# Cell passes of a four-layer graph network: visits past a group's second, one at a time with one-hots 128 wide

## The chip, the cores and the metric

The kernel runs on one core of a Trainium2 chip. The metric is the device time of one execution in microseconds (us).

## The reference

Four graph layers follow each other on 12,500 nodes with 64 features and 200,000 edges sorted by destination; each adds its result to `x`. Every layer gathers the rows of the edges' sources and sums them by destination. Layer 2 (GraphSAGE) does it twice, layer 3 (GCN) once, and these three sums are the subject here:

```python
dst = jnp.minimum((12500 * jax.random.uniform(..., (200000,)) ** 2.0).astype(jnp.int32), 99999)
# sorted; src goes along
...
def _sage_layer(h, src, dst, W_self, W_neigh, b, n_nodes):
    msg = h[src]
    agg = jax.ops.segment_sum(msg, dst, num_segments=n_nodes)
    deg = jax.ops.segment_sum(jnp.ones((src.shape[0], 1), h.dtype), dst, num_segments=n_nodes)
    h_neigh = agg / jnp.maximum(deg, 1.0)
    return h @ W_self + h_neigh @ W_neigh + b
...
msg = norm[:, None] * h[row]                             # layer 3
agg = jax.ops.segment_sum(msg, col, num_segments=N)
```

Since the destinations follow a square law, low nodes have many edges each and high nodes few.

## The kernel before

Layers 0 and 1 are worked by two edge passes, then `cells_setup` sorts the edges of each group by source page, and three **cell passes** (`cell_pass`) do the sums of layers 2 and 3. A cell pass goes over 75 groups (`CELLS`) of 2,688 edges. The nodes are cut into 98 windows of 128. A group has 26 tiles of 128 edge slots: 25 filled by a gather with one-hot matrices from `split` in SBUF, and one (`spill`) fetched by GpSimd's indirect DMA.

For each window that a group's destinations touch there is one **visit**: TensorE (PE) multiplies 26 one-hot tiles (slot by node of the window) with the 26 tiles of gathered rows (192 columns, a value split in three bf16 parts) into one PSUM bank (`segment`, line 1216), and VectorE (DVE) reduces the three parts (`reduce_visit`, line 1223) and adds them to the window of `agg` (`add_visit`, line 1228). Cutting the sorted destinations of the reference into groups of 2,688 gives in each pass 15 groups with one visit, 28 with two, 27 with three and 5 with four: 172 visits. The groups with three or four stand in the later part of the pass: counted from 0, groups 51 to 73 all have at least three. The five with four are groups 62, 66, 69, 71 and 73.

The one-hots are made on DVE by `build`: one small instruction for the places (line 1308), then 25 (`SLOT_TILES`) comparisons with fp8 output (line 1312) and one with bf16 output for the spill tile (line 1314). `lanes` counts from 0 to 255, so one build is 256 wide and serves two neighbouring windows, `half` 0 and 1. Buffers 0 and 1 hold the one-hots for a group's first and second visit, in turn by group; buffer 2 those for its third and fourth. In the first cell pass (`make`) DVE builds buffers 0 and 1 and SyncE (SP) stores them to HBM (`pairs_d`); the other two passes load them from there. Buffer 2 is always built anew.

Each engine has its own loop over the groups, two groups to an iteration (`over_rounds`), with the group's words in registers: `low` and `end` (the windows), `more` (the extra visits of all groups before) and `pairs`, from the table `sched`. The order on DVE for group g is: buffer 2 for g if `low + 2 < end`; in the first pass, the one-hots of group g+1; then the first visit's reduce and add, the second's under `If(low + 1 < end)`, and a `Fori` over the others in steps of two. PE works through the gather of group g+1 and the first visit of group g tile by tile in turn (line 1370 and line 1216), then the second visit, then its own `Fori`. The visits write PSUM banks in this way: the first `ps_first[k]`, the second and the fourth `ps_extra[0]`, the third `ps_extra[1]`. ScalarE (ACT) moves gathered rows from PSUM to SBUF (line 1286).

PE's third visit waits for `s_hot_more` (buffer 2 is built) and `s_add_more` (the bank is reduced); its fourth waits for `s_add_more` alone, since its one-hots lie in the other half of buffer 2.

Of the kernel before, what the change touches and what calls it, by code (L numbers as in the profile page):

```python
# [23 lines left out]
ALU = mybir.AluOpType  # L24
# [3 lines left out]
P = 128  # L28
NODES, EDGES, D = 12500, 200000, 64
WINDOWS = -(-NODES // P)  # L30
# [47 lines left out]
def build(nc, a):  # L78

    ctx = ExitStack()  # L80
    with ctx:
# [96 lines left out]
        def reach(eng, s, value):  # L178

            hold(eng, s, value & COUNTS)  # L180
# [580 lines left out]
        def cells_setup():  # L761
# [62 lines left out]
            with nc.Block() as block:  # L824
# [18 lines left out]
                def _(dve):  # L843
# [24 lines left out]
                    link(nc.vector.tensor_copy(extra[:, 0:1], high))  # L868
                    link(nc.vector.tensor_scalar(high, high, 1, 1, ALU.logical_shift_right, ALU.logical_shift_left))
                    link(nc.vector.tensor_copy(extra[:, 1:2], high))  # L870

# [259 lines left out]
        def cell_pass(start=None, bring=False, make=True):  # L1131
# [40 lines left out]
            def ranged(eng, regs, donate=True):  # L1172

                most = CELLS * (WINDOWS + 1)
                return (eng.snap(regs[0], donate=donate, min_val=0, max_val=WINDOWS - 1),
                        eng.snap(regs[1], donate=donate, min_val=1, max_val=WINDOWS),
                        eng.snap(regs[2], donate=donate, min_val=1 - WINDOWS, max_val=most),
                        eng.snap(regs[3], donate=donate, min_val=1 - WINDOWS, max_val=most))

            def over_rounds(eng, body):  # L1180
# [4 lines left out]
                def words():  # L1185

                    low, end, more, pairs = ranged(eng, regs[0:SCHED], False)
                    return low, end, more, pairs, eng.snap(regs[SCHED], min_val=0, max_val=WINDOWS - 1)

# [40 lines left out]
            with nc.Block() as block:  # L1230
# [62 lines left out]
                def _(dve):  # L1293
# [11 lines left out]

                    def build(k, g, w, placed, n_placed, signal):

                        nc.vector.tensor_scalar(place[k], slot_dst[:, bass.ds(g * SLOTS_OF, SLOTS_OF)], first[:, bass.ds(w, 1)],  # L1308
                                                1.0, ALU.subtract, ALU.subtract).then_inc(placed, 2)
                        reach(dve, placed, n_placed)  # L1310
                        for q in range(SLOT_TILES):
                            nc.vector.tensor_scalar(slots_hot[k][:, q, :], lanes[:, :], place[k][:, q:q + 1], None,  # L1312
                                                    ALU.is_equal, saturate=False)
                        last = nc.vector.tensor_scalar(spill_hot[k], lanes[:, :], place[k][:, SLOT_TILES:SLOTS_OF], None,
                                                       ALU.is_equal)
                        last.then_inc(signal, 2)

                    def add_up(of, w, k, added, signal, count):

                        reach(dve, s_add, added)  # L1320
                        reduce_visit(of, k).then_inc(signal, 1)
                        reach(dve, signal, count)
                        add_visit(w, k).then_inc(s_add, 1)

                    def body(it, r, words, following):
                        g0 = it * CELL_STEP
                        g = g0 + r
                        low, end, more, pairs, low1 = words
                        if there(it, r, 0):
                            with dve.If(low + 2 < end):  # L1330
                                build(2, g, low + 2, s_place_more, pairs + (low + 2), s_hot_more)
                        if there(it, r, 1):
# [13 lines left out]
                        with dve.If(low + 2 < end):  # L1346
                            with dve.Fori(low + 2, end, 2) as w:
                                reach(dve, s_sum_more, more + w)
                                add_up(ps_extra[1], w, 0, (more + w) + g, s_add_more, more + (w + 2))
                                with dve.If(w + 1 < end):  # L1350
                                    reach(dve, s_sum_more, more + (w + 1))
                                    add_up(ps_extra[0], w + 1, 1, (more + w) + (g0 + (r + 1)), s_add_more, more + (w + 3))
                                with dve.If(w + 2 < end):
                                    build(2, g, w + 2, s_place_more, pairs + (w + 2), s_hot_more)
                    over_rounds(dve, body)

                @block.tensor
                def _(pe):
# [17 lines left out]
                    def body(it, r, words, following):  # L1376
                        g0 = it * CELL_STEP
                        k = r % 2
                        low, end, more, pairs, _ = words
                        for c in range(n_pick):  # L1380
# [24 lines left out]
                        with pe.If(low + 2 < end):  # L1405
                            with pe.Fori(low + 2, end, 2) as w:
                                reach(pe, s_hot_more, pairs + w)
                                reach(pe, s_add_more, more + w)
                                segment(ps_extra[1], 2, 0, picked[k], rows_of, every).then_inc(s_sum_more, 1)
                                with pe.If(w + 1 < end):  # L1410
                                    reach(pe, s_add_more, more + (w + 1))
                                    segment(ps_extra[0], 2, 1, picked[k], rows_of, every).then_inc(s_sum_more, 1)

# [598 lines left out]
```

## Time and profile before

| | us |
|---|---|
| median of 3 runs | 10334.19 |
| lowest, highest | 10326.15, 10350.14 |
| the profiled execution | 10342.89 |
| its span | 10341.2 |
| DVE busy | 4747.4 |
| PE busy | 5394.1 |
| granted TensorE clock, mean | 0.681 |

The span runs from the first instruction of the program to the last. The three cell passes are roughly the stretches 7304 to 8395, 8495 to 9320 and 9475 to 10305 us of it. A busy share is a mean over stages with different limits, so what one stage is bound by is read from that stage's own rows.

### The profile page before, as it was taken

How to read it: one execution, taken by the hardware profiler on the slowest of the kernel's cores; microseconds unless marked ns; L12 is line 12 of the kernel's file. 1: busy time of each engine (PE TensorE's matmuls, PEld its weight loads, DVE VectorE, ACT ScalarE, POOL GpSimd, SP SyncE). 2: the span in 40 equal slices, each digit the busy share in tenths (PEclk: the TensorE clock that was granted, in tenths of full speed). 3: DMA queues.
4: the chain of work that ended last, by engine and by line, in shares of the span. 5: the costliest groups of instructions: out<-in, count | busy, mean ns of one | idle time of the engine just before them, and what ended most of it. 6: DMA issues, size and time to landing. Idle time of an engine off the chain costs nothing. (4 is left out here: it accounts for less than half of the span.)

```text
span 10341.2 us, 263147 instructions
## 1 busy us (share of the span) xinstructions
PE 5394.1 (52%) x94327; PEld 4139.3 (40%) x94328; DVE 4747.4 (46%) x12946; ACT 1982.3 (19%) x3084; POOL 3376.8 (33%) x3400
## 2 busy tenths in 40 slices
PE   1333233333344444444444456666776668885886
PEld 1222222222233333333333355555454455664565
DVE  3333333333533333333333377777778751463156
ACT  1111111111211111111111100000443225433542
POOL 4666666665144444444444400000111100000000
PEclk7555555555655555555555567777798879996999
DMA  2221122211122222222222112223332124322432
GB/s 74 48 47 48 47 48 49 47 47 41 35 57 59 59 59 59 59 59 60 60 59 59 49 51 81 83 82 97 117 117 79 67 76 140 122 95 104 137 116 100
DMA packets 310309, 747.47 MB, mean 72 GB/s; under 512 B 85284, under 2 KB 110500, under 8 KB 307225
## 3 DMA queue, kind: packets, MB, share of 16 engines
q1 hardware_dynamic: 175524, 610.42, 18.1%
q0 software_dynamic: 107552, 114.03, 5.5%
q10 hardware_dynamic: 26656, 16.06, 0.5%
q8 instruction: 272, 4.46, 0.2%
q14 instruction: 305, 2.50, 0.1%
HBM read 601.52 MB, written 138.69 MB: 72 GB/s over the span
## 5 line engine op out<-in xcount | busy, mean ns | idle before, releaser
L556 POOL DMA_INDIRECT store<-table,store x3136 | 3071.9, 980 | 2623.4 <-DVE store L689 1660.9
L709 PE MATMUL ps_all<-store 128*128 128x65 bf16 (+1 forms) x18816 | 1493.5, 232 | 3027.6 <-issue 2705.8
L709 PEld LDWEIGHTS ps_all<-store 128*128 128x128 bf16 x18816 | 1094.1, 122 | 3386.0 <-issue 3382.8
L1216 PE MATMUL ps_all<-store 128*128 128x192 bf16 x13416 | 1505.6, 254 | 382.3 <-DVE turned L1223 175.5
L637 DVE TENSOR_TENSOR agg<-ps_all,agg 128x130 f32 (+1 forms) x392 | 113.7, 290 | 3128.2 <-PE ps_all L709 2361.0
L1286 ACT CAST store<-ps_all 128x768 bf16<-128x768 f32 x1350 | 1063.8, 799 | 1575.6 <-PE ps_all L1370 1526.3
L1216 PEld LDWEIGHTS ps_all<-store 128*128 128x128 fp8e4 x13416 | 1074.9, 100 | 722.1 <-issue 698.7
L1312 DVE TENSOR_SCALAR store<-lanes,turned 128x256 fp8e4<-128x256 bf16 x4275 | 1138.2, 347 | 26.9 <-DVE turned L1308 21.8
L1244 POOL DMA_INDIRECT store<-table_b,spill_row x225 | 297.1, 1320 | 2277.8 <-PE ps_all L1370 2119.7
L731 PE MATMUL ps_all<-wide,store 128*128 x9408 | 538.1, 241 | 458.1 <-DVE store L644 413.3
L731 PEld LDWEIGHTS ps_all<-wide,store 128*128 128x128 bf16 x9408 | 505.4, 131 | 490.0 <-issue 489.8
L628 DVE TENSOR_SCALAR store<-lanes,place_of 128x256 bf16<-128x256 bf16 x3136 | 665.6, 297 | 62.9 <-DVE place_of L624 51.0
L1223 DVE TENSOR_REDUCE turned<-ps_all 128x64 f32<-128x192 f32 x516 | 183.1, 355 | 913.4 <-PE ps_all L1216 846.9
L600 ACT ACTIVATE store<-store 128x512 bf16<-128x512 f32 x196 | 125.2, 639 | 2163.3 <-DVE store L681 2162.0
L422 POOL MEMSET wide<- 128x384 bf16 x4 | 1.7, 418 | 1573.5 <-POOLq L1088 1216.7
L1370 PE MATMUL ps_all<-wide,store 128*32 128x192 bf16 x11172 | 413.8, 265 | 154.6 <-issue 72.9
L594 ACT CAST store<-store 128x512 bf16<-128x512 f32 x392 | 244.3, 623 | 1121.6 <-issue 686.4
L1370 PE MATMUL ps_all<-wide,turned 128*32 128x192 bf16 x10878 | 405.7, 266 | 99.1 <-issue 77.8
L644 DVE TENSOR_SCALAR store<-store,node_id 128x1024 bf16<-128x1024 int32 x392 | 277.3, 749 | 171.8 <-issue 133.3
L1370 PEld LDWEIGHTS ps_all<-wide,store 128*32 128x32 fp8e4 x11172 | 230.7, 100 | 302.3 <-issue 301.4
L1370 PEld LDWEIGHTS ps_all<-wide,turned 128*32 128x32 fp8e4 x10878 | 227.2, 101 | 246.1 <-issue 245.6
L603 ACT CAST store<-store 128x512 bf16<-128x512 f32 x196 | 122.6, 625 | 967.6 <-DVE store L684 797.7
(229 smaller groups left out, 5405.6 us busy)
## 6 DMA issues: line engine op xcount, KB each, us to landing
store<-pairs_d SPq DMA_DIRECT2D x150, 864.0 KB, 4.5
store<-in_dst_rows SPq DMA_DIRECT2D x196, 512.0 KB
pairs_d<-store SPq DMA_DIRECT2D x75, 864.0 KB, 4.0
store<-lows_d SPq DMA_DIRECT2D x75, 784.0 KB, 5.2
store<-in_edge_attr SPq DMA_DIRECT2D x196, 256.0 KB
store<-table,store POOLq DMA_INDIRECT x3136
store<-cells_d SPq DMA_DIRECT2D x114, 392.0 KB
turned<-cells_d SPq DMA_DIRECT2D x111, 392.0 KB
```

What stands on the lines that cost most here:

```text
L556: nc.gpsimd.indirect_dma_start(rows_f[:, g % SLOTS, j, :], None, table, bass.IndirectOffsetOnAxis(ap=src[:, g * TILES + j:g * TILES + j + ...
L594: nc.scalar.copy(value[slot][:, :, 1, 0:D], rows_f[:, slot, :, :]).then_inc(s_mid, 1)
L628: last = nc.vector.tensor_scalar(onehots[:, k, j, :], lanes[:, :], place[:, j:j + 1], None, ALU.is_equal)
L644: nc.vector.tensor_scalar(onehot_t[b][:, :, :].rearrange("p j e -> p (j e)"), side_i[:, slot, :], node_id[:, bass.ds(w + b, 1)], None, ALU ...
L709: last = nc.tensor.matmul(ps_pair[r % 2][:, b * width:(b + 1) * width], onehot[r % 2][b][:, j, :], value[r][:, j, i, 0:width], start=(b == ...
L731: last = nc.tensor.matmul(ps_hid[:, r % 2, j * D:(j + 1) * D], onehot_t[b][:, j, :], split[:, bass.ds(w + b, 1), i, :].rearrange("p o d -> ...
L1216: last = nc.tensor.matmul(to, hot[:, half * P:(half + 1) * P], rows[:, q, :] if q < SLOT_TILES else spill, start=(q == 0), stop=True, skip ...
L1223: return nc.vector.tensor_reduce(sums[k], of.rearrange("p (i d) -> p d i", i=PARTS), AX.X, ALU.add)
L1244: nc.gpsimd.indirect_dma_start(spill[:, g, :], None, table_b, bass.IndirectOffsetOnAxis(ap=spill_row[:, g:g + 1], axis=0)).then_inc(s_fetc ...
L1286: nc.scalar.copy(picked[r % 2][:, c * PICK:(c + 1) * PICK, :], of).then_inc(s_evicted, 1)
L1312: nc.vector.tensor_scalar(slots_hot[k][:, q, :], lanes[:, :], place[k][:, q:q + 1], None, ALU.is_equal, saturate=False)
L1370: last = nc.tensor.matmul(ps_pick[(r + 1 + c) % 2][j * CAP:(j + 1) * CAP, q, 0:PARTS * D], gather_hot[k][:, w * CAP:(w + 1) * CAP], split[ ...
```

## The change

Visits past the second are worked one by one. `build` takes a width: with `n=1` each of its 26 comparisons makes 128 columns in place of 256, for one window. On DVE, buffer 2 is built so for the third visit, and after the add of visit `w` it is built again for `w + 1` if there is one. All visits past the second use the bank `ps_extra[1]` and `half` 0. The `Fori` of both engines goes in steps of one, PE's loop has no `If` inside, and DVE's has one in place of two. The word `pairs` becomes `lone`, a count of such visits, and `cells_setup` works it out in one instruction fewer.

```diff
--- before.py
+++ after.py
@@ -866,8 +866,7 @@
                     link(nc.vector.tensor_scalar(columns[:, 1:2], high, 1.0, None, ALU.add))
                     link(nc.vector.tensor_tensor(high, high, low, ALU.subtract))
                     link(nc.vector.tensor_copy(extra[:, 0:1], high))
-                    link(nc.vector.tensor_scalar(high, high, 1, 1, ALU.logical_shift_right, ALU.logical_shift_left))
-                    link(nc.vector.tensor_copy(extra[:, 1:2], high))
+                    link(nc.vector.tensor_scalar(extra[:, 1:2], extra[:, 0:1], 1.0, 0.0, ALU.subtract, ALU.max))
 
             s_target = sem("s_c_target")
             s_cell, s_sums, s_summed, s_prefix, s_top, s_over, s_rank, s_rank_hot, s_slots = (sem(f"s_c_{n}") for n in (
@@ -1184,8 +1183,8 @@
 
                 def words():
 
-                    low, end, more, pairs = ranged(eng, regs[0:SCHED], False)
-                    return low, end, more, pairs, eng.snap(regs[SCHED], min_val=0, max_val=WINDOWS - 1)
+                    low, end, more, lone = ranged(eng, regs[0:SCHED], False)
+                    return low, end, more, lone, eng.snap(regs[SCHED], min_val=0, max_val=WINDOWS - 1)
 
                 def following(it, r):
                     def load():
@@ -1303,17 +1302,17 @@
                         nc.vector.memset(agg[:, WINDOWS:PAIR_END, :], 0.0)
                         nc.vector.tensor_copy(agg[:, 0:WINDOWS, 0:D], start[:, :, :]).then_inc(s_add, 1)
 
-                    def build(k, g, w, placed, n_placed, signal):
+                    def build(k, g, w, placed, n_placed, signal, n=2):
 
                         nc.vector.tensor_scalar(place[k], slot_dst[:, bass.ds(g * SLOTS_OF, SLOTS_OF)], first[:, bass.ds(w, 1)],
-                                                1.0, ALU.subtract, ALU.subtract).then_inc(placed, 2)
+                                                1.0, ALU.subtract, ALU.subtract).then_inc(placed, n)
                         reach(dve, placed, n_placed)
                         for q in range(SLOT_TILES):
-                            nc.vector.tensor_scalar(slots_hot[k][:, q, :], lanes[:, :], place[k][:, q:q + 1], None,
+                            nc.vector.tensor_scalar(slots_hot[k][:, q, 0:n * P], lanes[:, 0:n * P], place[k][:, q:q + 1], None,
                                                     ALU.is_equal, saturate=False)
-                        last = nc.vector.tensor_scalar(spill_hot[k], lanes[:, :], place[k][:, SLOT_TILES:SLOTS_OF], None,
-                                                       ALU.is_equal)
-                        last.then_inc(signal, 2)
+                        last = nc.vector.tensor_scalar(spill_hot[k][:, 0:n * P], lanes[:, 0:n * P],
+                                                       place[k][:, SLOT_TILES:SLOTS_OF], None, ALU.is_equal)
+                        last.then_inc(signal, n)
 
                     def add_up(of, w, k, added, signal, count):
 
@@ -1325,10 +1324,10 @@
                     def body(it, r, words, following):
                         g0 = it * CELL_STEP
                         g = g0 + r
-                        low, end, more, pairs, low1 = words
+                        low, end, more, lone, low1 = words
                         if there(it, r, 0):
                             with dve.If(low + 2 < end):
-                                build(2, g, low + 2, s_place_more, pairs + (low + 2), s_hot_more)
+                                build(2, g, low + 2, s_place_more, lone + (low + 1), s_hot_more, 1)
                         if there(it, r, 1):
                             if make:
                                 k = (r + 1) % 2
@@ -1344,14 +1343,11 @@
                             reach(dve, s_sum_more, more + (low + 1))
                             add_up(ps_extra[0], low + 1, 1, (more + low) + (g0 + (r + 1)), s_add_more, more + (low + 3))
                         with dve.If(low + 2 < end):
-                            with dve.Fori(low + 2, end, 2) as w:
+                            with dve.Fori(low + 2, end) as w:
                                 reach(dve, s_sum_more, more + w)
-                                add_up(ps_extra[1], w, 0, (more + w) + g, s_add_more, more + (w + 2))
+                                add_up(ps_extra[1], w, 0, (more + w) + (g0 + (r + 1)), s_add_more, more + (w + 2))
                                 with dve.If(w + 1 < end):
-                                    reach(dve, s_sum_more, more + (w + 1))
-                                    add_up(ps_extra[0], w + 1, 1, (more + w) + (g0 + (r + 1)), s_add_more, more + (w + 3))
-                                with dve.If(w + 2 < end):
-                                    build(2, g, w + 2, s_place_more, pairs + (w + 2), s_hot_more)
+                                    build(2, g, w + 1, s_place_more, lone + w, s_hot_more, 1)
                     over_rounds(dve, body)
 
                 @block.tensor
@@ -1376,7 +1372,7 @@
                     def body(it, r, words, following):
                         g0 = it * CELL_STEP
                         k = r % 2
-                        low, end, more, pairs, _ = words
+                        low, end, more, lone, _ = words
                         for c in range(n_pick):
                             if there(it, r, 1):
                                 gather(it, r, c)
@@ -1403,13 +1399,10 @@
                             reach(pe, s_add_more, more + (low + 2))
                             segment(ps_extra[0], k, 1, picked[k], rows_of, every).then_inc(s_sum_more, 1)
                         with pe.If(low + 2 < end):
-                            with pe.Fori(low + 2, end, 2) as w:
-                                reach(pe, s_hot_more, pairs + w)
-                                reach(pe, s_add_more, more + w)
+                            with pe.Fori(low + 2, end) as w:
+                                reach(pe, s_hot_more, lone + (w - 1))
+                                reach(pe, s_add_more, more + (w + 1))
                                 segment(ps_extra[1], 2, 0, picked[k], rows_of, every).then_inc(s_sum_more, 1)
-                                with pe.If(w + 1 < end):
-                                    reach(pe, s_add_more, more + (w + 1))
-                                    segment(ps_extra[0], 2, 1, picked[k], rows_of, every).then_inc(s_sum_more, 1)
 
                     over_rounds(pe, body)
```

The rows below are instructions in the order of the program on one engine. Line numbers are each kernel's own: 1308, 1312 and 1314 of before (places, fp8 and bf16 comparisons) are 1307, 1311 and 1313 of the change, 1216 is 1215, and 1223 and 1228 are 1222 and 1227. The first two pieces are DVE's loop over the visits past the second, from the last add in it to the loop's end. Before:

```order
L1228 TENSOR_TENSOR agg<-turned,agg 128x64
L1350 UNCONDITIONAL_BRANCH
L1353 COMPARE_AND_BRANCH
L1308 ISA
L1308 TENSOR_SCALAR turned<-wide,first 128x26
L175 REGISTER_ALU x2
L1312 TENSOR_SCALAR store<-lanes,turned 128x256 x25
L1314 TENSOR_SCALAR store<-lanes,turned 128x256
L1353 UNCONDITIONAL_BRANCH
L1347 REGISTER_ALU
L1347 COMPARE_AND_BRANCH
```

And of the change, from the only add in the loop:

```order
L1227 TENSOR_TENSOR agg<-turned,agg 128x64
L1349 REGISTER_ALU
L1349 COMPARE_AND_BRANCH
L1307 ISA
L1307 TENSOR_SCALAR turned<-wide,first 128x26
L175 REGISTER_ALU x2
L1311 TENSOR_SCALAR store<-lanes,turned 128x128 x25
L1313 TENSOR_SCALAR store<-lanes,turned 128x128
L1349 UNCONDITIONAL_BRANCH
L1346 REGISTER_ALU
L1346 COMPARE_AND_BRANCH
```

Two branches, each with a jump of its own, stood behind the third visit's add (L1350 ahead of the fourth visit, L1353 ahead of a build for a fifth and sixth); one is left (L1349), and the build behind it is 128 wide and is now reached for a fourth visit.

The same loop on PE, before (L1370 is the next group's gather, L1410 the inner condition):

```order
L1405 COMPARE_AND_BRANCH
L1406 UNCONDITIONAL_BRANCH
L1406 ISA
L175 REGISTER_ALU x3
L1216 MATMUL ps_all<-store 128x192 x26
L1410 REGISTER_ALU
L1410 COMPARE_AND_BRANCH
L175 REGISTER_ALU x2
L1216 MATMUL ps_all<-store 128x192 x26
L1410 UNCONDITIONAL_BRANCH
L1406 REGISTER_ALU
L1406 COMPARE_AND_BRANCH
```

And of the change:

```order
L1401 COMPARE_AND_BRANCH
L1402 UNCONDITIONAL_BRANCH
L1402 ISA
L175 REGISTER_ALU
L175 ISA
L175 REGISTER_ALU
L1215 MATMUL ps_all<-store 128x192 x26
L1402 REGISTER_ALU
L1402 COMPARE_AND_BRANCH
```

One block of 26 matmuls is left, with the loop's branch right behind it; a fourth visit goes round the loop and waits for both semaphores again.

## Rows read from the trace of the kernel before

**Rows 1.** The page's head: the span.

```profile
span 10341.2 us, 263147 instructions
```

**Rows 2.** Busy us (x instructions) of PE, PEld, DVE, ACT, POOL; clock; DMA; GB/s.

```profile
7304.00:8395.00 1091.00, 769.61 (x11778) 536.39 (x11774) 851.51 (x3234) 379.54 (x524) 151.56 (x72) 0.87 0.27 91
8495.00:9320.00 825.00, 686.77 (x11632) 490.41 (x11628) 324.25 (x1208) 368.42 (x515) 63.36 (x68) 0.97 0.36 117
9475.00:10305.00 830.00, 688.76 (x11668) 491.88 (x11665) 324.27 (x1208) 370.29 (x516) 63.37 (x68) 0.97 0.36 117
```

**Rows 3.** Timeline, first cell pass, three-visit groups: start, us, engine, line [idle before].

```profile
8094.30 0.35 DVE L1223 TENSOR_REDUCE turned<-ps_all 128x64 f32<-128x192 f32 x1
...
8099.59 0.24 DVE L1308 TENSOR_SCALAR turned<-wide,first 128x26 f32 x1 [1.87 <-issue]
...
8106.75 0.23 DVE L1308 TENSOR_SCALAR turned<-wide,first 128x26 f32 x1
...
8113.90 0.34 DVE L1223 TENSOR_REDUCE turned<-ps_all 128x64 f32<-128x192 f32 x1
```

**Rows 4.** Timeline, second cell pass, three-visit groups, DVE and PE.

```profile
9091.50 2.31 PE L1216 MATMUL ps_all<-store 128*128 128x192 bf16 x26 [0.81 <-DVE store L1314]
...
9093.99 0.51 PE L1370 MATMUL ps_all<-wide,turned 128*32 128x192 bf16 x16 [0.18 <-issue]
...
9094.94 0.23 DVE L1228 TENSOR_TENSOR agg<-turned,agg 128x64 f32 x1 [0.24 <-DVE turned L1223]
...
9097.12 0.24 DVE L1308 TENSOR_SCALAR turned<-wide,first 128x26 f32 x1 [1.95 <-issue]
...
9104.09 0.28 DVE L1314 TENSOR_SCALAR store<-lanes,turned 128x256 bf16<-128x256 bf16 x1
...
9104.88 2.31 PE L1216 MATMUL ps_all<-store 128*128 128x192 bf16 x26 [1.17 <-DVE store L1314]
```

**Rows 5.** Waits of PE for the builds, second pass, then third: us, times, longest.

```profile
PE ps_all L1216 <- DVE store L1314: 24.3, 22, 1.5
...
PE ps_all L1216 <- DVE store L1314: 22.2, 22, 1.4
```

**Rows 6.** Timeline, second cell pass, a group with four visits.

```profile
9157.07 4.45 PE L1216 MATMUL ps_all<-store 128*128 128x192 bf16 x52 [1.17 <-DVE store L1314]
...
9160.40 0.23 DVE L1228 TENSOR_TENSOR agg<-turned,agg 128x64 f32 x1 [0.24 <-DVE turned L1223]
...
9161.45 0.51 PE L1370 MATMUL ps_all<-wide,store 128*32 128x192 bf16 x16
```

**Rows 7.** Timeline, first cell pass, a group with four visits.

```profile
8154.30 4.32 PE L1216 MATMUL ps_all<-store 128*128 128x192 bf16 x26 [5.96 <-DVE turned L1223]
...
8155.79 0.23 DVE L1228 TENSOR_TENSOR agg<-turned,agg 128x64 f32 x1 [0.24 <-DVE turned L1223]
...
8159.63 0.23 DVE L1228 TENSOR_TENSOR agg<-turned,agg 128x64 f32 x1 [0.24 <-DVE turned L1223]
```

**Rows 8.** Busy and clock while that group's fourth visit runs.

```profile
8154.20:8158.60 4.40, 4.30 (x30) 3.72 (x34) 0.81 (x3) 0.00 (x0) 0.00 (x0) 0.50 0.69 242
```

**Rows 9.** Durations by line (ns min/median/max), whole run; L959 is of the setup.

```profile
L1312 DVE TENSOR_SCALAR store<-lanes,turned x4275: 334/347/492, 7305.8 to 10287.3; 128x256 fp8e4<-128x256 bf16 x195
...
L1314 DVE TENSOR_SCALAR store<-lanes,turned x171: 270/279/327, 7312.5 to 10287.6; 128x256 bf16<-128x256 bf16 x171
...
L959 DVE TENSOR_SCALAR store<-store,next_id x75: 1845/1853/1855, 6088.8 to 7217.2; 128x3136 fp8e4<-128x3136 bf16 x75
```

**Rows 10.** Branches: DVE's at one group's end in the second pass; PE's, whole run.

```profile
L1353 DVEq COMPARE_BRANCH  x1: 123/123/123, 9095.4 to 9095.4; - x1
...
L1347 DVEq ALU_OP  x1: 45/45/45, 9095.8 to 9095.8; - x1
...
L1330 DVEq ALU_OP  x1: 40/40/40, 9096.7 to 9096.7; - x1
...
L1405 PEldq COMPARE_BRANCH  x225: 71/216/1780, 7322.3 to 10297.6; - x113
```

## The prediction

> **What bounds the kernel now.** The page's head gives the span, 10341.2 us [rows 1]; the profiled execution took 10342.89, the median of the three runs is 10334.19. The change touches the three cell passes alone, so I first read the busy times of those three stretches [rows 2]: 1091, 825 and 830 us long. In the first DVE is busy for 852 us, in the other two PE for 687 and 689 and DVE for only 324. So the same edit has two different backgrounds.
>
> In the first pass the timeline of DVE [rows 3] shows two builds end to end (8099.59 to 8106.75 and on to 8113.9) and a period of 8113.90 - 8094.30 = 19.60 us in three-visit groups. The one large gap, 1.87, is "issue": branches and register work, no wait for PE. DVE sets this pass, and a us off its builds is a us off the pass.
>
> In the other two passes a period is 9104.88 - 9091.50 = 13.38 us [rows 4]. Here the chain goes through both engines: PE's third visit starts when the build has ended (9104.09 + 0.28 = 9104.37, PE at 9104.88: 0.51 later), DVE adds it at 9094.94, reaches its next build 2.18 us later at 9097.12, and builds for 7.25 us. But PE idles only 0.81 and 1.17 us for it. What a faster build can give here is bounded by that idle time, not by the build. The waits of PE for L1314 are 24.3 us in 22 times in the second pass and 22.2 in 22 in the third [rows 5].
>
> **The narrower build.** A comparison with fp8 output takes 347 ns for 256 columns; the same kind of instruction over 3,136 columns takes 1853 [rows 9]. That is 1506/2880 = 0.523 ns a column, so most of the 347 is not columns: 128 fewer take off 67 ns, not half. The bf16 one takes 279, which is 68 less for the same 256 columns, so its columns cost half as much: 33 ns off. One build: 25 x 67 + 33 = 1.71 us less, 7.25 becomes 5.54. No row has an fp8 comparison 128 wide. The bounds are no saving at all, and half of the distance between starts (7.16 us for the 27 instructions of a build in rows 3 is 0.265 each), 3.4 us a build. I take 1.71, because two independent row pairs give the same slope. The Trainium skill ("VectorE: DVE Perf Modes", section on the TRN2 errata) speaks against cutting builds up: a fixed cost is paid per instruction whatever its size. The trace agrees as to the kind (0.523 ns a column under a 347 ns instruction of 256). The page's formula, 58 cycles + columns over the mode's factor, would make 128 fp8 columns 127 ns; that is an estimate from the page, and by it the whole sum would be some 26 us lower, since each fourth build would be 1.7 us shorter. The rows' fixed part is larger than that, and the rows decide.
>
> There are 32 such builds a pass. **First pass:** 32 x 1.71 = 54.7 us off. The second branch behind the add goes too: L1353 starts at 9095.4, the next record at 9095.8 [rows 10], I take 0.35: 32 x 0.35 = 11.2 off. PE does not become the bound there: it idles for DVE by several us a group.
>
> **Second and third pass:** PE's idle time before third visits vanishes. Each listed wait is under the 1.71 (longest 1.5), so all of 46.5 us in 44 waits goes, and a little more: 52 matmuls of two visits with no wait between take 4.45 us [rows 6], 26 take 2.31, so an unhindered visit starts 0.17 before the modelled end of the one ahead: 44 x 0.17 = 7.5. The other 20 waits are too short to be listed; I estimate 0.3 each, 6. Together 60 off. PE's inner condition costs something only in every second group: the next gather starts 0.18 after the third visit's end [rows 4], against 0.07 before the end where no jump is taken (9161.45 against 9157.07 + 4.45) [rows 6]: 27 x 0.25 = 7 off. Then PE alone is the bound.
>
> **The fourth visit.** Five groups a pass lose what the wide build gave them: one-hots ready for the fourth visit. Now the chain is: third add, a build, PE, the add, with nothing beside it, and PE's queue holds the whole next group behind its wait.
>
> *First pass.* Before, the third add starts at 8155.79 and the fourth at 8159.63: 3.84 [rows 7]. After: from the add to the build 0.48 (register work begins with the add, and L1330's, at 9096.7, leads to L1308 at 9097.12 [rows 4, 10]), the build 5.54, hand-over to PE 0.51, the visit 4.32, to the add 1.01 (8154.30 + 4.32 to 8159.63 [rows 7]): 11.86. That is 8.0 more, 5 x 8.0 = 40. PE's lateness hides behind the two builds that follow. First pass in all: -54.7 - 11.2 + 40 = -25.9.
>
> *Second and third.* Before, with the third visit at S = 9157.07, the next gather starts at S + 4.38 and the third add at S + 3.33 [rows 6]. After: fourth visit on PE at S + 3.33 + 0.48 + 5.54 + 0.51 = S + 9.86. By then PE has idled 7.5 us. In the first pass an idle time of 5.96 us was followed by a visit of 4.32 us [rows 7] at a granted clock of 0.50 [rows 8], that is at 1.2 GHz, where one at 2.4 GHz takes 2.31. So I take the low level here too, though these passes now hold 0.97 in the mean [rows 2]: 4.32 - 0.16 of overlap, and 0.25 for the gather's first tiles. The next gather starts at S + 14.3, 9.9 late; PE is the bound, so nothing hides it: 10 x 9.9 = 99.
>
> **The sum.** -25.9 - 60 - 7 + 99 = +6 us against the profiled 10342.89, and as much against the median: 10334 + 6 = 10340. The rest (one setup instruction less, fewer words of program) is nothing. Three numbers of opposite signs nearly cancel, so the forecast is no change that can be measured.
>
> **Rivals.**
> *PE gets back less than its idle time (slower).* A gather starts 0.18 us after a third visit with nothing but branches ahead of it [rows 4]. If a third visit kept that gap behind the second in place of 0.17 of overlap, 64 x 0.35 = 22 of the 60 stay lost: +28, 10362. Against it: with only the bank to wait for, two visits ran with no gap [rows 6]. Chance 0.14. It decides once more than 0.23 a visit stays lost.
> *The loop's back edge stalls (slower).* The loop now goes round, 15 times on each engine. A branch of PE took up to 1780 ns [rows 10]. At that price on the chain: 15 x 1.7 = 25, 10365. Against it: the median branch is 216 ns, and PE's sequencer meets the back edge while it must wait for the build anyway. The Trainium skill ("Runtime: NRT & Kernel Launch", section on instruction fetch) says that a taken branch to a page outside the fetched window stalls for a fetch; no row here tells where pages lie. Chance 0.09.
> *The narrow comparison is not shorter in spacing (slower).* Then 54.7 + 60 are not gained and 15 builds cost 1.7 more: 6 + 115 + 25 = +146, 10480. Two row pairs speak against it. Chance 0.04.
> *The fourth visit is cheaper (faster).* If PE stays at 2.4 GHz in its fourth visits, 15 x 2.2 = 33 fall away: -27, 10307. If the spacing halves, 47 builds are 1.7 shorter where it counts: -78, 10260. The clock rows speak against the first, the slope against the second. Chance 0.14.
>
> **How the numbers follow.** The sum as worked out has a chance of 0.59, and by its own terms lies within 25 us of 10340. A change of 0.2% (21 us) is about what this measurement can tell from none. Of the 0.59, 0.46 lies within that, 0.10 above, 0.03 below. With the rivals: faster 0.03 + 0.12 = 0.15; slower 0.10 + 0.12 + 0.07 + 0.04 = 0.33; same 0.52. The range reaches down to the clock rival and up past the two small slow ones, with the runs' own scatter (10326 to 10350): 10305 to 10385; beyond lie the two builds' extremes.
>
> **What the next profile should show.** L1311 at 280 ns and L1313 near 246, 200 ns apart; the first pass 26 us shorter, the second and third 14 and 18 longer, between them three-visit periods of some 12 us with PE never idle for a build, and in the 10 four-visit groups a hole of 7.5 us on PE with 0.50 behind it. Wrong would be: PE still idle before third visits, no hole or a longer one, or a first pass as long as before.

## The result

| | us |
|---|---|
| median of the changed kernel, 4 runs | 10512.73 |
| lowest, highest | 10505.1, 10526.6 |
| median of the kernel before beside it, 4 runs | 10342.17 |
| ratio, 95% interval | 1.0168, 1.0149 to 1.0186 |
| span of the profiled execution | 10503.4 (before 10341.2) |

The change makes the kernel slower by 1.7%, some 170 us, where no change was forecast. These are the three cell passes of the changed kernel, with the busy us of each engine as in [rows 2]:

```profile
7300.00:8480.00 1180.00, 770.63 (x11782) 553.53 (x11774) 824.42 (x3369) 377.19 (x524) 75.29 (x72) 0.84 0.25 84
8580.00:9450.00 870.00, 695.94 (x11649) 497.59 (x11638) 299.50 (x1345) 368.82 (x515) 63.45 (x68) 0.95 0.35 113
9603.00:10468.00 865.00, 688.54 (x11647) 493.64 (x11644) 297.21 (x1343) 369.58 (x515) 63.45 (x68) 0.96 0.34 112
```

DVE is busy for less in each pass (824 against 852, 300 against 324, 297 against 324), and yet each is longer. I measure a pass from its first add of a visit to its last. These are the adds of before, first pass, and of the changed kernel's three passes (count, ns, first and last start in us):

```profile
L1228 DVE TENSOR_TENSOR agg<-turned,agg x172: 224/226/295, 7323.1 to 8389.3; 128x64 f32 x172
```

```profile
L1227 DVE TENSOR_TENSOR agg<-turned,agg x172: 224/226/293, 7319.4 to 8474.6; 128x64 f32 x172
...
L1227 DVE TENSOR_TENSOR agg<-turned,agg x172: 224/226/291, 8583.9 to 9443.4; 128x64 f32 x172
...
L1227 DVE TENSOR_TENSOR agg<-turned,agg x172: 224/226/230, 9607.4 to 10462.2; 128x64 f32 x172
```

So the passes take 1155.2, 859.5 and 854.8 us, against 1066.2, 817.7 and 819.2 before: +89, +42 and +36, 166 together, where the spans differ by 162. Forecast were -26, +14 and +18.

The timeline of the first pass shows where the time goes. Here is a group with three visits, DVE and PE (beside [rows 3]):

```profile
8064.73 0.24 DVE L1313 TENSOR_SCALAR store<-lanes,turned 128x128 bf16<-128x128 bf16 x1
8064.90 0.23 DVE L1307 TENSOR_SCALAR turned<-wide,first 128x26 f32 x1
...
8073.27 0.36 DVE L1222 TENSOR_REDUCE turned<-ps_all 128x64 f32<-128x192 f32 x1 [0.42 <-DVE agg L1227]
...
8073.78 3.80 PE L1215 MATMUL ps_all<-store 128*128 128x192 bf16 x26 [6.92 <-DVE turned L1222]
...
8078.00 0.36 DVE L1222 TENSOR_REDUCE turned<-ps_all 128x64 f32<-128x192 f32 x1 [3.89 <-PE ps_all L1215]
```

The narrow one-hots are ready at 8064.97, and PE's third visit starts at 8073.78. What releases it is DVE's second reduce at 8073.27, which stands behind the build of the next group's one-hots. By then PE has idled 6.92 us, the third visit takes 3.80 us in place of 2.31, and DVE waits 3.89 for it, in a pass in which DVE is the bound. All 32 third visits of this pass look like that: PE idles 6.6 to 8.3 us ahead of each and takes 3.6 to 4.3 for it. The second pass has the same wait in small, beside [rows 4]:

```profile
9160.03 2.31 PE L1215 MATMUL ps_all<-store 128*128 128x192 bf16 x26 [0.39 <-issue]
9160.74 0.25 DVE L1313 TENSOR_SCALAR store<-lanes,turned 128x128 bf16<-128x128 bf16 x1
...
9162.60 0.36 DVE L1222 TENSOR_REDUCE turned<-ps_all 128x64 f32<-128x192 f32 x1 [0.87 <-PE ps_all L1215]
9163.10 1.07 PE L1215 MATMUL ps_all<-store 128*128 128x192 bf16 x11 [0.76 <-DVE turned L1222]
```

The build is over at 9160.99, before PE is done with the second visit at 9162.34, as forecast; but PE idles 0.76 us all the same, again until a second reduce. These are PE's waits of the second pass, as in [rows 5]:

```profile
PE ps_all L1215 <- DVE store L1313: 37.4, 5, 7.5
PE ps_all L1366 <- ACT store L1285: 24.7, 57, 0.6
PE ps_all L1215 <- DVE turned L1222: 24.4, 32, 0.8
```

The 22 waits for a build are gone; 5 are left, those of the fourth visits, 7.5 us each. In their place stand 32 waits for L1222, one for each third visit, 24.4 us, as much as before.

The reason is in the diff, and the prediction went past it. `s_add_more` begins at 2 and counts the reduces of all extra visits (those past a group's first), and `more + low` is the number of those of earlier groups. PE's third visit, w = low + 2, waited for `more + w`, which needs nothing of its own group. In the change it waits for `more + (w + 1)`: one reduce of its own group, the second visit's. The one bank does not ask for that, since the second visit has another. (A second count in the diff moves by one as well: DVE's third reduce now waits for the second visit's add, where `(more + w) + g` was the first visit's. That one costs nothing: from the second add to the third reduce it is 8039.24 - 8038.45 = 0.79 us before and 8164.03 - 8163.24 = 0.79 in e1 below, which has the new count.)

### The profile page after: what moved, and what is told of

It is laid out like the page before. It is cut to its first block and busy times, and to the rows that moved or that the text cites. A ratio compares the mean times of both kernels' runs of the same rounds, so it can differ in the third digit from the quotient of the medians.

```text
span 10503.4 us, 263458 instructions
## 1 busy us (share of the span) xinstructions
PE 5394.3 (51%) x94327; PEld 4158.3 (40%) x94328; DVE 4665.0 (44%) x13350; ACT 1980.2 (19%) x3084; POOL 3287.3 (31%) x3400
## 5 line engine op out<-in xcount | busy, mean ns | idle before, releaser
L1215 PE MATMUL ps_all<-store 128*128 128x192 bf16 x13416 | 1546.6, 259 | 534.7 <-DVE turned L1222 309.1
L1215 PEld LDWEIGHTS ps_all<-store 128*128 128x128 fp8e4 x13416 | 1117.1, 102 | 873.4 <-issue 841.7
L1311 DVE TENSOR_SCALAR store<-lanes,turned 128x128 fp8e4<-128x128 bf16 (+1 forms) x4650 | 1053.0, 306 | 29.0 <-DVE turned L1307 23.6
L1243 POOL DMA_INDIRECT store<-table_b,spill_row x225 | 220.8, 981 | 2431.6 <-PE ps_all L1366 2273.3
L1222 DVE TENSOR_REDUCE turned<-ps_all 128x64 f32<-128x192 f32 x516 | 183.2, 355 | 1182.8 <-PE ps_all L1215 1155.0
```

The lines of the kernel that those rows point to most:

```text
L1215: last = nc.tensor.matmul(to, hot[:, half * P:(half + 1) * P], rows[:, q, :] if q < SLOT_TILES else spill, start=(q == 0), stop=True, skip ...
L1222: return nc.vector.tensor_reduce(sums[k], of.rearrange("p (i d) -> p d i", i=PARTS), AX.X, ALU.add)
L1243: nc.gpsimd.indirect_dma_start(spill[:, g, :], None, table_b, bass.IndirectOffsetOnAxis(ap=spill_row[:, g:g + 1], axis=0)).then_inc(s_fetc ...
L1311: nc.vector.tensor_scalar(slots_hot[k][:, q, 0:n * P], lanes[:, 0:n * P], place[k][:, q:q + 1], None, ALU.is_equal, saturate=False)
```

## The experiments

Ratios are to runs of the kernel before beside each experiment: median 10385.4 us for e1, e2, e3 and e6, and 10333.0 for e4, e5 and e7. The two sets differ outside the cell passes: there (the span less the three passes) the profiled executions of before, the changed kernel, e4, e5 and e7 spend 7633 to 7638 us, those of the other four 7678 to 7694. So the passes are compared, measured as above.

| kernel | ratio to before | 95% interval | passes, us |
|---|---|---|---|
| before | | | 1066.2, 817.7, 819.2 |
| the changed kernel | 1.0168 | 1.0149 to 1.0186 | 1155.2, 859.5, 854.8 |
| e1_loose_wait | 0.9988 | 0.9978 to 0.9999 | 1040.0, 835.0, 829.0 |
| e2_tight_wait | 1.0186 | 1.0169 to 1.0202 | 1179.1, 859.7, 860.2 |
| e3_narrow_by_need | 0.9932 | 0.9918 to 0.9947 | 1042.9, 798.0, 798.3 |
| e4_busy_before_fourth | 0.9986 | 0.9977 to 0.9995 | 1036.7, 826.9, 823.8 |
| e5_busy_before_third | 1.0120 | 1.0104 to 1.0136 | 1102.9, 861.8, 861.6 |
| e6_no_fifth | 0.9961 | 0.9946 to 0.9975 | 1060.9, 807.0, 809.5 |
| e7_narrow_two_branches_less | 0.9929 | 0.9915 to 0.9943 | 1033.8, 792.3, 796.5 |

A pass differs by 2 to 7 us even where a run changes nothing in it (e5's second and third against the changed kernel's). The period of a group is steadier: from the start of the last add of one group to that of the next, worked out from the 172 adds of each pass, mean of groups 51 to 73 (18 with three visits, 5 with four), in us for the first, second and third pass:

| kernel | three visits | four visits |
|---|---|---|
| before | 19.18, 12.91, 12.80 | 23.00, 15.07, 15.04 |
| the changed kernel | 20.70, 12.67, 12.68 | 32.33, 23.85, 23.90 |
| e1_loose_wait | 17.23, 11.80, 11.78 | 28.81, 23.20, 23.26 |
| e2_tight_wait | 22.90, 14.36, 14.40 | 25.44, 16.56, 16.50 |
| e3_narrow_by_need | 18.16, 11.95, 11.93 | 23.10, 15.25, 15.22 |
| e4_busy_before_fourth | 17.23, 11.76, 11.72 | 27.20, 21.24, 21.31 |
| e5_busy_before_third | 19.07, 12.67, 12.69 | 30.88, 23.95, 24.06 |
| e6_no_fifth | 18.85, 12.49, 12.45 | 22.72, 14.64, 14.66 |
| e7_narrow_two_branches_less | 17.85, 11.81, 11.84 | 23.00, 14.87, 14.86 |

### The wait alone taken back: e1_loose_wait

Against the changed kernel:

```diff
                                 reach(pe, s_hot_more, lone + (w - 1))
-                                reach(pe, s_add_more, more + (w + 1))
+                                reach(pe, s_add_more, more + w)
```

> The changed kernel with one edit: in TensorE's loop over the visits past the second, the wait on s_add_more is for more + w instead of more + (w + 1), so a third visit no longer waits until the group's second visit has been reduced (a fourth is still held back until the third is reduced, by the wait for its one-hots). Theory (the extra wait is what the prediction missed): all other terms of the prediction then hold, +6 us on the kernel before, ratio 1.000 within 0.003; first pass about 26 us shorter than before's 1066, second and third 14 and 18 longer than 818 and 819, and no idle time of TensorE before third visits in those two. Rival (the extra fourth builds and the low clock behind them are the loss): the time stays within 30 us of the changed kernel, ratio at 1.013 or more.

Measured: 0.9988. The first pass is 26.2 us shorter than before (forecast 25.9), the second and third are 17.3 and 9.8 longer (forecast 14 and 18). On the timeline, a third visit of the second pass:

```profile
9109.70 0.24 DVE L1307 TENSOR_SCALAR turned<-wide,first 128x26 f32 x1 [1.51 <-issue]
9110.09 4.99 DVE L1311 TENSOR_SCALAR store<-lanes,turned 128x128 fp8e4<-128x128 bf16 x25 [0.16 <-DVE turned L1307]
...
9114.33 4.45 PE L1215 MATMUL ps_all<-store 128*128 128x192 bf16 x52 [0.34 <-issue]
9115.00 0.24 DVE L1313 TENSOR_SCALAR store<-lanes,turned 128x128 bf16<-128x128 bf16 x1
```

Second and third visit run as one block of 52 matmuls. The theory stands and its rival falls: a count that is off by one is the whole loss. Pass by pass the changed kernel is 115, 25 and 26 us over e1, together 166.

### The wait alone put in: e2_tight_wait

Against the kernel before:

```diff
                                 reach(pe, s_hot_more, pairs + w)
-                                reach(pe, s_add_more, more + w)
+                                reach(pe, s_add_more, more + (w + 1))
```

> The kernel before with only the opposite edit: its third visit waits for more + (w + 1), that is for the reduce of the second visit. One-hots, banks and loops stay as before. Theory of the extra wait: in the first pass VectorE then waits some 3.6 us in each of 32 groups for a third visit that starts only after its second reduce, +115 us; in the others TensorE's third visit starts 1.5 us later on the chain, 32 x 1.5 = +48 each; together +210, ratio 1.020. Rival: ratio within 0.003 of 1.

Measured: 1.0186. The passes are 113, 42 and 41 us longer, 196 together (forecast 115, 48 and 48); a three-visit group of the second pass takes 1.45 us more (forecast 1.5). In the first pass, with wide one-hots and two banks:

```profile
8073.35 0.36 DVE L1223 TENSOR_REDUCE turned<-ps_all 128x64 f32<-128x192 f32 x1 [0.42 <-DVE agg L1228]
8073.86 4.32 PE L1216 MATMUL ps_all<-store 128*128 128x192 bf16 x26 [9.24 <-DVE turned L1223]
8073.96 0.23 DVE L1228 TENSOR_TENSOR agg<-turned,agg 128x64 f32 x1 [0.25 <-DVE turned L1223]
8078.60 0.36 DVE L1223 TENSOR_REDUCE turned<-ps_all 128x64 f32<-128x192 f32 x1 [4.41 <-PE ps_all L1216]
```

It is the same picture as in the changed kernel: the loss needs neither the narrow build nor the single bank nor the new loop.

### The narrow build where there is no fourth visit: e3_narrow_by_need

Against the kernel before (`build` takes the width `n` as in the change):

```diff
                             with dve.If(low + 2 < end):
-                                build(2, g, low + 2, s_place_more, pairs + (low + 2), s_hot_more)
+                                with dve.If(low + 3 < end):
+                                    build(2, g, low + 2, s_place_more, pairs + (low + 2), s_hot_more)
+                                with dve.If(end < low + 4):
+                                    build(2, g, low + 2, s_place_more, pairs + (low + 2), s_hot_more, 1)
```

> The kernel before, where buffer 2 is built 128 wide if the group has three visits and 256 wide, as before, if it has four. The banks, waits and the fourth visit are those of before. It has what the narrow build gives without the second build: first pass 27 x 1.71 = 46 us off, less some 0.4 us of branches in each of 32 groups, other passes 27/32 of 60 = 50 off: -83, ratio 0.992. If the narrow build is worth nothing on the chain: 1.001.

Measured: 0.9932. Each pass is shorter, by 23, 20 and 21 us: 64, where 83 were forecast (33 in the first, 50 in the others). On the first pass's timeline, first e3, then the kernel before:

```profile
8055.97 0.24 DVE L1308 TENSOR_SCALAR turned<-wide,first 128x26 f32 x1 [2.53 <-issue]
...
8071.82 0.23 DVE L1228 TENSOR_TENSOR agg<-turned,agg 128x64 f32 x1 [0.24 <-DVE turned L1223]
8074.02 0.24 DVE L1308 TENSOR_SCALAR turned<-wide,first 128x26 f32 x1 [1.97 <-issue]
8074.41 4.99 DVE L1312 TENSOR_SCALAR store<-lanes,turned 128x128 fp8e4<-128x128 bf16 x25
...
8079.48 0.23 DVE L1308 TENSOR_SCALAR turned<-wide,first 128x26 f32 x1
```

```profile
8041.34 0.24 DVE L1308 TENSOR_SCALAR turned<-wide,first 128x26 f32 x1 [1.27 <-issue]
```

The build takes 8079.48 - 8074.02 = 5.46 us to the next, as it should. What is off in the first pass is the branches. The gap ahead of the build takes two values in turn, 1.97 and 2.53 here, against 1.27 and 1.87 before. That is 0.7 for two conditions and a jump over a build, not 0.4: 32 x 0.7 = 22 of the 46 that the narrow builds gain are spent again. A three-visit group takes 1.02 us less, the 1.71 of the build less 0.7. In the other passes it takes 0.96 and 0.87 less (forecast 60 / 64 = 0.94), and a four-visit group, whose wide build starts later too, 0.18 more. That the two passes together gain 41 us in place of 50 is thus for the most part not in these groups; its cause is not shown. This kernel is faster than the one before and than the changed one.

### TensorE kept busy ahead of the fourth visit: e4_busy_before_fourth

Against e1. A spare visit is 26 matmuls whose sums nobody reads:

```diff
                             with pe.Fori(low + 2, end) as w:
+                                with pe.If(low + 2 < w):
+                                    reach(pe, s_add_more, more + w)
+                                    for _ in range(3):
+                                        segment(ps_extra[0], k, 1, picked[k], rows_of, every)
                                 reach(pe, s_hot_more, lone + (w - 1))
                                 reach(pe, s_add_more, more + w)
```

> The kernel of e1_loose_wait, where TensorE does three spare visits (78 matmuls whose sums nobody reads, into the second visit's bank, already reduced) right after the third visit of a four-visit group, while VectorE builds the one-hots for the fourth. Theory (the clock falls in the hole of 7.5 us): with 6.4 us of it filled, the fourth visits of the second and third pass take 2.31 us instead of some 4.1, and each of these two passes is some 11 us shorter than in e1 (835, 829); the first pass stays, since there the spare work is over long before. Ratio some 0.002 below e1's. Rival (the hole alone costs, not the clock): passes as in e1, visits of 4 us stay.

In e1 a fourth visit of the second pass starts after the hole that was forecast, and at half the clock:

```profile
9161.64 4.45 PE L1215 MATMUL ps_all<-store 128*128 128x192 bf16 x52 [0.40 <-issue]
9173.56 4.32 PE L1215 MATMUL ps_all<-store 128*128 128x192 bf16 x26 [7.47 <-DVE store L1313]
9177.80 0.83 PE L1366 MATMUL ps_all<-wide,store 128*32 128x192 bf16 x16
```

```profile
9173.60:9177.90 4.30, 4.30 (x30) 3.81 (x34) 0.00 (x0) 0.00 (x0) 0.00 (x0) 0.50 0.00 0
```

With the spare work, second, third and three spare visits run in one block, then the fourth:

```profile
9241.54 10.88 PE L1215 MATMUL ps_all<-store 128*128 128x192 bf16 x130 [0.33 <-issue]
9253.46 2.31 PE L1215 MATMUL ps_all<-store 128*128 128x192 bf16 x26 [1.03 <-DVE store L1313]
```

```profile
9241.50:9252.40 10.90, 10.86 (x130) 10.68 (x130) 7.57 (x37) 0.00 (x0) 0.00 (x0) 1.00 0.12 37
9253.40:9255.80 2.40, 2.34 (x34) 2.21 (x37) 0.00 (x0) 0.00 (x0) 0.00 (x0) 1.00 0.00 0
```

The granted clock stays at 1.00 (2.4 GHz) and the fourth visit takes 2.31 us, in all ten four-visit groups of the two passes. A four-visit group takes 1.96 and 1.95 us less than in e1, some 10 a pass (11 expected), while the three-visit groups stay within 0.06. The passes as a whole are 8 and 5 us shorter, which is near their scatter, and the whole time (0.9986 against 0.9988) cannot tell such a size.

The expectation for the first pass was wrong in its reason. The spare work is not over long before: it waits for the second visit's reduce, and so starts late and runs into the fourth visit. First e1, then e4:

```profile
8171.08 4.30 PE L1215 MATMUL ps_all<-store 128*128 128x192 bf16 x26 [13.94 <-DVE store L1313]
```

```profile
8190.20 10.38 PE L1215 MATMUL ps_all<-store 128*128 128x192 bf16 x104 [5.72 <-DVE turned L1222]
```

The 104 matmuls are the spare ones and the fourth visit. So a four-visit group is 1.6 us shorter there too (27.20 against 28.81), and the pass 3.

### TensorE kept busy ahead of the third visit: e5_busy_before_third

Against the changed kernel:

```diff
                                 reach(pe, s_hot_more, lone + (w - 1))
+                                if make:
+                                    with pe.If(w < low + 3):
+                                        reach(pe, s_add_more, more + w)
+                                        for _ in range(3):
+                                            segment(ps_extra[1], 2, 0, picked[k], rows_of, every)
                                 reach(pe, s_add_more, more + (w + 1))
```

> The changed kernel, extra wait and all, where in the first cell pass alone TensorE does three spare visits (sums nobody reads, into the bank that the third visit then starts anew) while it waits for the second visit's reduce. In the changed kernel it idles some 7 us there and its third visits then take 3.6 to 4.3 us at 1.2 GHz, and VectorE waits for them. If half of the first pass's loss is that clock: third visits of 2.31 us, first pass 32 x 1.6 = 51 us shorter, 1104, ratio 1.012. If only the order of the wait costs: first pass as before at 1155, ratio 1.017.

Measured: 1.0120, first pass 1102.9 (1104 was expected); the others, which this does not touch, 861.8 and 861.6, as in the changed kernel within 7 us.

```profile
8052.55 0.36 DVE L1222 TENSOR_REDUCE turned<-ps_all 128x64 f32<-128x192 f32 x1 [0.42 <-DVE agg L1227]
...
8053.05 2.31 PE L1215 MATMUL ps_all<-store 128*128 128x192 bf16 x26 [0.51 <-DVE turned L1222]
...
8055.78 0.36 DVE L1222 TENSOR_REDUCE turned<-ps_all 128x64 f32<-128x192 f32 x1 [2.40 <-PE ps_all L1215]
...
8062.67 8.74 PE L1215 MATMUL ps_all<-store 128*128 128x192 bf16 x104 [0.33 <-issue]
```

The last line is the next group's second visit and its three spare ones.

The clock during that third visit, in the changed kernel and then here:

```profile
8073.80:8077.50 3.70, 3.70 (x26) 3.31 (x26) 0.23 (x1) 0.00 (x0) 0.00 (x0) 0.58 0.78 273
```

```profile
8053.10:8055.40 2.30, 2.30 (x34) 2.14 (x38) 0.23 (x1) 0.00 (x0) 0.00 (x0) 1.00 0.95 308
```

The granted clock is 0.58 (mostly at 1.2 GHz, then back at 2.4) against 1.00, and all 32 third visits take 2.31 us. PE does 78 matmuls more a group, and the pass is 52 us shorter (a three-visit group 1.63). So of the 115 us that the wait costs in the first pass, 52 are the clock that falls while PE waits, and 63 the wait itself.

### One branch less on VectorE: e6_no_fifth, and both: e7_narrow_two_branches_less

Against the kernel before for e6, and the same two lines against e3 for e7:

```diff
-                                with dve.If(w + 2 < end):
-                                    build(2, g, w + 2, s_place_more, pairs + (w + 2), s_hot_more)
```

> The kernel before without the build for a fifth visit and its condition in VectorE's loop (no group of these inputs has a fifth). This is the branch that the change drops on VectorE: 32 x 0.35 = 11 us off in the first pass, nothing in the others, where TensorE waits for a build 0.35 earlier: up to 0.35 x 22 x 2 = 15 more. Ratio 0.9975 to 0.999. If the branch is hidden: 1.000.

Measured: 0.9961, that is 40 us, where 0.9975 to 0.999 was expected (the interval just reaches 0.9975). The passes are 5, 11 and 10 us shorter, 26 together, the most that was expected. This run changes nothing else, and where the other 14 come from is not shown, so I count the 26. By the periods the branch is worth 0.33 us a three-visit group in the first pass (0.35 was taken), and 0.42 and 0.35 in the others. Taking a branch of DVE away pays there too, since PE's third visit waits for the build behind it: the waits for L1314 in the second pass fall from 24.3 us [rows 5] to 11.8. First e6, then e3:

```profile
PE ps_all L1216 <- DVE store L1314: 11.8, 15, 1.1
```

```profile
PE ps_all L1216 <- DVE store L1314: 7.3, 5, 1.6
```

> The kernel of e3_narrow_by_need without the build for a fifth visit and its condition, as in e6_no_fifth. If both gains add up: the passes 64 + 25 = 90 us shorter than the kernel before's, ratio 0.990; if they draw on the same idle time of TensorE: first pass 11 shorter than e3's, the others as in e3, 0.992.

Measured: 0.9929, the same as e3 within its interval. The passes are 9, 6 and 2 us shorter than e3's, of which only the 9 is clear of their scatter. The periods say the same: a three-visit group is 0.31 us shorter in the first pass, where DVE is the bound, and 0.14 and 0.09 in the others. There the narrow build alone had used up nearly all the idle time of PE: e3 has 5 listed waits for L1314 left, those of the four-visit groups. So the two gains draw for the most part on the same idle time.

## Why the prediction was wrong

**The step that failed** is "PE does not become the bound there: it idles for DVE by several us a group", with its counterpart "PE's idle time before third visits vanishes". Both take PE's third visit as released by the build alone; the prediction says so outright ("with only the bank to wait for, two visits ran with no gap"). The row behind that [rows 6] shows a fourth visit behind a third, and that fourth waits for the second visit's reduce, one visit back. In the change the third waits for that same reduce, of the visit directly ahead of it. The diff had moved its other wait from `more + w` to `more + (w + 1)`. In the first pass this put the third visit behind DVE's next build, on the chain of the engine that is the bound: 115 us, 52 of them by the clock. In the others it put the second visit's reduce between two visits that would have run back to back: 0.76 + 0.17 of overlap = 0.93 a third visit, 32 x 0.93 = 30 us a pass by the rows, 25 and 26 by e1 (0.87 and 0.90 a three-visit group). No rival had it either; the first of them (PE gets back less than its idle time) named the place, but with branches as the cause and 0.35 a visit as the price, and for the two short passes alone. That PE idles for several us is no slack when what it waits for, and who waits for it next, are on the same chain.

**The rest held, as e1 shows** (sum of the passes +1 us, forecast +6; the ratio of 0.9988 would be -12, which the passes do not show). The sum is not right by chance alone, since its parts can be read from the periods. A three-visit group is 1.95 us shorter in the first pass (forecast 1.71 + 0.35 = 2.06), and 1.11 and 1.02 in the others (60 / 64 + 0.25 = 1.19). A four-visit group is 5.8 longer in the first (8.0 - 2.06 = 5.9), and 8.1 and 8.2 in the others (9.9 - 0.94 = 9.0). Gains and losses both came out a little smaller than forecast, and these errors cancel in part: so much of the agreement to 5 us is luck.

- The narrow build: 25 comparisons take 4.99 us and a build 5.53 (8059.44 of the changed kernel's first pass to 8064.97), against 5.54 taken from two slopes. The rival that nothing is saved and the one that half is are both out. By the formula of the Trainium skill ("VectorE: DVE Perf Modes", section on the TRN2 errata) a comparison would be 127 ns, an estimate from that page; the row has 4.99 us for 25, that is 0.20 each, and the measurement decides. It agrees with the page as to the kind: a fixed cost per instruction that narrowing does not touch.
- PE's idle before third visits: all the listed waits are gone in e1, and a three-visit period on PE is 9161.64 - 9149.78 = 11.86 us, where some 12 were forecast.
- The fourth visit in e1: third add to build 8165.03 - 8164.63 = 0.40 (forecast 0.48), hole of 7.47 in the second pass (7.5), visit of 4.0 to 4.3 us at a granted clock of 0.50 to 0.56 (4.32 at 0.50). In the second pass the third visit starts at S = 9161.64 + 2.14 = 9163.78 and the next gather at 9177.80, S + 14.0, that is 9.6 late (S + 14.3 and 9.9). In the first pass it is 8176.40 - 8164.63 = 11.77 from the third add to the fourth (11.86).
- The back edge costs nothing that shows: in the hole of 7.47 and at DVE's 0.40 there is no room for it.
- The second branch: 0.33 us a group in the first pass by e6 (0.35 taken).
- The sum's parts do cancel: without the second build, e3 gains 64 us; with it, e1 gains nothing. The two parts of the diff that are worth having are the width and the branch, and the one that eats them is the second build in 5 groups of 75.

One slip in the prediction has no effect: in the rival with half the spacing, 47 x 1.7 = 80 us make -74, as its 10260 has it, and not -78.

## What to carry to other kernels

When a loop is rewritten, write down for each wait which event its number stands for, before and after, and price every one that comes to stand for a later event; a count that is one too high still gives the same sums and shows only as time. An engine's idle time is slack only if what it waits for is not made by the engine that waits for it. And a cheap form (128 wide, half the columns) that a few cases can't use is better chosen by case: made by need it gained 0.7%; forced on the five groups of a pass in which it must be made twice, it gained nothing.

## What the runs showed of the hardware

Useless matmuls shortened a pass: in e5, 78 spare ones in each of 32 groups kept the granted clock at 1.00 where PE otherwise idles some 7 us, and took 52 us off 1155. The third visits behind them took 2.31 us in place of 3.6 to 4.3.

An fp8 comparison on DVE starts 0.20 us after the one ahead of it at 128 columns and 0.26 at 256 (4.99 and 6.65 us for 25, with the last one's own 0.28 and 0.35 in it), so halving the width takes a quarter off.
